# Second attention: high and low parts of queries and keys stacked on the 32 rows of one single-pass product, spread by transfers into three buffers

## The chip, the cores and the metric

The kernel runs on one core of one Trainium2 chip. The metric is the device time of one execution in microseconds; lower is better. The engines named below are TensorE (PE; its weight loads are shown apart as PEld), VectorE (DVE), ScalarE (ACT), GpSimd (POOL) and SyncE (SP), which here only issues transfers.

## The reference, cut to what matters

The whole program is two transformer-like layers over 8 batches of 256 tokens of width 128. The change touches the attention of the second layer alone:

```python
H, HD, R, QK = 16, 8, 8, 32
xn = _ln(x, g1, b1)
q = _lin(xn, Wq, bq).reshape(b, n, H, HD) / np.sqrt(HD)
k = _lin(xn, Wk, bk).reshape(b, n, H, HD)
score = jax.nn.softmax(jnp.einsum('bihd,bjhd->bhij', q, k), axis=-1)
v = _lin(xn, Wv, bv).reshape(b, n, R, HD)
out = jnp.einsum('bhij,bjrd->bihrd', score, v)
comp = softmax([qv, out] @ Ws.T + bs, axis=3)      # over the 8 value heads
out = (comp * out).sum(axis=3)
```

There are 16 query heads of only 8 features. So a score product contracts over 8 numbers, while the array has 128 rows.

## The kernel before, in words

The program is a row of stages; a barrier of all engines stands between two of them. The stage in question (here "the second attention") begins at about 584.7 us and ends at about 834 us of the profile. The stage ahead of it is that of the mixture of experts (from 453 us) with the layer norms that follow it (to 584 us).

**Heads and rows.** `Q` holds the projected queries of a batch, 128 rows by 256 tokens: four groups of 32 rows, each with the 8 features of four heads. `KZ` holds the keys four times, each copy with only one head of every group left and the others made zero (scale and bias columns `QT`, `BS`, L1276 to L1279). A score product of head k takes the 32 rows `rows_of(k)` (group k % 4) of `Q` and of copy k // 4 of `KZ`, so it contracts over 32 rows of which 8 count. All these operands are plain float32; every such matmul appears in the profile as two instructions. `MR`, `SEL` are rounded float32 (fp32r) and a matmul of them is one instruction.

**Two products per head.** L2164 ("max") computes the scores with queries on the partitions; DVE takes the maximum over the keys from it (L2312). L2161 ("exp") computes them transposed, and L2169 subtracts the maximum in the same bank (`SEL` picks the head's row of `MR`); ACT takes the exponential into `PT` (L2225). L2201 then multiplies the four 128x128 pieces of `PT` of each head by `VXT` (64 value columns, 8 score columns, a column of ones); ACT copies the result to `UB` (L2238).

**The order of the work** is written out by hand and is the same on each engine (`batches`, `turn`). A batch has eight steps i = 0 to 7. In step i PE issues `scores(i)`: the exp products of heads 2i, 2i+1 of batch b and the max products of two heads of batch b+1, interleaved; after it, from i = 1 on, `weighted(i - 1)`, the 16 instructions of L2201 for two heads. After step 7 come `project_next` (queries and keys of batch b+2 from `TR` and `WQK`, L1270; ACT then makes `Q` and `KZ`), `weighted(6)`, `turn_max` (two transposes of `M4`, L2186, which DVE copies to `MR`, L2326) and `weighted(7)`. A first round with no batch to finish (`b = None`) does the maxima of batch 0 only; the last one has no maxima. DVE, besides the maxima, does for the batch before the "finish" steps: start (step 0), end (step 2, after ACT's exponential of `CM`, L2245), weigh (steps 3, 4, L2293) and sum (steps 5, 6, L2299). After the last maximum of a batch DVE rounds and splits the maxima (`MH`, `M4`, L2316 to L2320), which `turn_max` waits for.

**Banks.** `UP_` (banks 0 to 3: max, projection, turn) and `UM` (banks 4 to 7: exp, weighted) are rings: a use waits until the engine that reads the use four places earlier is done. `keep_busy` (L295) issues identity products on PE: three ahead of the first scores, four after the first `turn_max`.

**The stage ahead of it** folds the norm's gain and shift into `WQK` and the bias columns (L1913 to L1950), and in its last waves ACT and DVE run norms by turns, after which PE turns, projects values (L1852) and projects batch 0 (L1270); ACT makes `Q`, `KZ` of batch 0 as its last work there (L1909).

Of the kernel before, what the change touches and what calls it, by code (L numbers as in the profile page):

```python
# [21 lines left out]
P = 128  # L22
# [151 lines left out]
def build(nc, x_in, pa_in, pb_in, pc_in, pd_in, out_dram):  # L174
# [4 lines left out]
    with ctx:  # L179
# [1076 lines left out]
        s4 = ctx.enter_context(ExitStack())  # L1256
        VXT = sbuf(s4, "VXT", [P, NT, VX])
        CT = sbuf(s4, "CT", [P, NT, H2])
        BS = sbuf(s4, "BS", [P, 5])
# [3 lines left out]
        Q = [sbuf(s4, f"Q{n}", [P, L]) for n in range(2)]  # L1263
        KZ = [sbuf(s4, f"KZ{n}", [P, 4, L]) for n in range(2)]
# [9 lines left out]
        def take_projections(bank, odd):  # L1274

            nc.scalar.activation(Q[odd][:, :], bank[:, 0:L], ACT.Identity, bias=BS[:, 4:5], scale=1.0 / math.sqrt(HD2))  # L1276
            for s_ in range(4):
                last = nc.scalar.activation(KZ[odd][:, s_, :], bank[:, L:2 * L], ACT.Identity, bias=BS[:, s_:s_ + 1],
                                            scale=QT[:, s_:s_ + 1])  # L1279
            return last  # L1280

        sb = ExitStack()
        with sb:
# [440 lines left out]
            sba.close()  # L1724
            XBT = sbuf(sb, "XBT", [P, SLOTS * P])
# [11 lines left out]
            BX = sbuf(sb, "BX", [P, 2])  # L1737
            PROD = sbuf(sb, "PROD", [P, 4 * 64])
# [11 lines left out]
            c_turned, c_copied, c_proj, c_qk0 = sem("c_turned"), sem("c_copied"), sem("c_proj"), sem("c_qk0")  # L1750
# [20 lines left out]
            with nc.Block() as block:  # L1771
                @block.sync
                def _(sp):
                    sp.wait_ge(moe_stored, 16 * SLOTS)
                    for g in range(NG):
                        own = slice(4 * g, 4 * g + 4)
                        sp.dma_start(MO[:, own, :], by_token[0:NT * P, :].rearrange("(t p) c -> p t c", p=P)[:, own, :])\
                            .then_inc(moe_back[g], 16)

                @block.gpsimd  # L1780
                def _(pool):
                    nc.gpsimd.memset(BD[:, :, :], 0.0).then_inc(c_zero, 1)
                    nc.gpsimd.memset(VXT[:, :, VX - 1:VX], 1.0).then_inc(c_zero, 1)
                    pool.wait_ge(loadC, 16)
                    for n, w in enumerate(("wq", "wk")):
                        nc.gpsimd.tensor_copy(WQK[:, n * P:(n + 1) * P].rearrange("p (j s d) -> p j s d", j=4, s=4),
                                              one_part(pc(w))).then_inc(c_wqk, 1)
# [9 lines left out]
                def _(pe):  # L1797
# [3 lines left out]
                    last.then_inc(c_cols, 1)  # L1801
                    pe.wait_ge(c_bd, 1)
# [41 lines left out]
                    pe.wait_ge(c_ready, 2)  # L1844
                    for g in range(NG):
# [10 lines left out]
                        if g == 0:  # L1856
                            project(PS[:, 0, :], 0).then_inc(c_qk0, 1)

                @block.scalar
                def _(act):  # L1860
# [49 lines left out]
                    act.wait_ge(c_qk0, 1)  # L1910
                    take_projections(PS[:, 0, :], 0)

                @block.vector  # L1913
                def _(dve):
# [13 lines left out]
                    V.link(nc.vector.tensor_copy(SEL[:, :], CRW[:, :]))  # L1928
                    dve.wait_ge(c_cols, 1)
# [833 lines left out]
```

## Time and profile before

| what | us |
|---|---|
| times of three runs | 1008.54 (median), 1008.1, 1018.52 |
| the profiled execution, its own time | 1008.61 |
| its span, first to last instruction | 1006.9 |
| the second attention, steps of batches 0 to 7 | 608.5 to 823.2 |
| mean granted TensorE clock over the span | 0.813 |

The span leaves out 1.7 us of the profiled execution's time. Busy time of an engine is the union of its instructions. In a line of the timeline, several instructions of one kind in a row are merged (xN); "[idle before <- releaser]" is how long the engine had waited and what ended it. The granted clock is 1.0 at 2.4 GHz and 0.5 at 1.2 GHz.

### The profile page before, as it was taken

The numbers are of one execution on the slowest core, as the hardware profiler recorded it, in microseconds if no ns is written. First come the engines' busy times: TensorE is split into PE (matmuls) and PEld (weight loads), VectorE is DVE, ScalarE is ACT, GpSimd is POOL, SyncE is SP. The second block draws the span as 40 slices with busy tenths as digits, with TensorE's granted clock in tenths as the row PEclk, the third lists the DMA queues.
The fourth block names the chain that finished last, engine by engine and source line by source line (L and its number), as shares of the span: only waits on it lengthen the run. The fifth ranks groups of instructions, "written<-read, shape, count | busy, mean of one in ns | idle before, by whom it ended". The sixth has DMA issues, their size and how long they took to land. (4 is left out here: it accounts for less than half of the span.)

```text
span 1006.9 us, 15707 instructions
## 1 busy us (share of the span) xinstructions
PE 742.9 (74%) x5853; PEld 608.8 (60%) x5853; DVE 589.5 (59%) x1330; ACT 446.8 (44%) x920; POOL 84.6 (8%) x96
## 2 busy tenths in 40 slices
PE   3993869998932695518940479999999974759986
PEld 2443769995432475418840347888888864538765
DVE  4119999983484363413327543777777657575574
ACT  3332526453534454203534614555555533446554
POOL 0002203000001101061420020000000001000000
PEclk9996757697955788557985569999999986869989
DMA  5200260005001000021020030000000000000000
GB/s 166 33 0 1 41 105 1 1 3 220 26 1 64 1 1 1 1 68 46 31 63 0 0 118 1 2 2 1 0 1 1 2 1 1 0 1 1 1 22 21
DMA packets 27457, 26.43 MB, mean 26 GB/s; under 512 B 17424, under 2 KB 25488, under 8 KB 26624
## 3 DMA queue, kind: packets, MB, share of 16 engines
q1 hardware_dynamic: 26144, 22.99, 8.0%
q0 software_dynamic: 1248, 2.57, 0.8%
q8 instruction: 42, 0.69, 0.3%
q14 instruction: 23, 0.19, 0.1%
HBM read 20.32 MB, written 5.23 MB: 25 GB/s over the span
## 5 line engine op out<-in xcount | busy, mean ns | idle before, releaser
L2201 PE MATMUL PS<-VXT,PT 128*128 128x73 f32 (+1 forms) x1024 | 126.6, 277 | 4.8 <-ACT PT L2225 4.8
L2201 PEld LDWEIGHTS PS<-VXT,PT 128*128 128x128 f32 x1024 | 119.7, 192 | 17.0 <-issue 12.3
L2312 DVE TENSOR_REDUCE MX<-PS 128x2 f32<-128x512 f32 x128 | 81.7, 686 | 47.5 <-PE PS L2164 46.8
L2225 ACT ACTIVATE PT<-PS 128x512 f32<-128x512 f32 x128 | 68.6, 597 | 47.4 <-PE PS L2169 47.4
L2161 PE MATMUL PS<-Q,KZ 32*128 32x256 f32 x512 | 76.8, 397 | 0.0
L2164 PE MATMUL PS<-KZ,Q 32*128 32x256 f32 x512 | 72.8, 409 | 1.9 <-DVE MX L2312 1.7
L2169 PE MATMUL PS<-MR,SEL 32*128 32x256 f32 x256 | 58.8, 462 | 0.0
L2238 ACT ACTIVATE UB<-PS 128x292 f32<-128x292 f32 x64 | 26.6, 415 | 52.8 <-PE PS L2201 52.8
L2164 PEld LDWEIGHTS PS<-KZ,Q 32*128 32x128 f32 x512 | 45.1, 190 | 5.3 <-DVE MX L2312 4.1
L404 PE MATMUL PS<-XT,WT 128*128 x96 | 42.3, 595 | 1.0 <-ACT XT L290 1.0
L2161 PEld LDWEIGHTS PS<-Q,KZ 32*128 32x128 f32 x512 | 38.8, 184 | 5.7 <-issue 0.8
L1876 ACT ACTIVATE HT<-PS,PB 128x128 f32<-128x128 f32 x92 | 26.2, 368 | 24.9 <-PE PS L1834 20.8
L2538 ACT ACTIVATE PB<-PS,PB 128x512 f32<-128x512 f32 x48 | 31.8, 685 | 4.2 <-PE PS L2451 4.2
L2642 DVE TENSOR_TENSOR HBL<-PB,HBH 128x512 fp32r<-128x512 f32 x32 | 22.1, 692 | 19.3 <-ACT PB L2538 18.8
L2293 DVE TENSOR_TENSOR UP<-UB,CM 128x1024 f32<-128x1024 f32 x16 | 32.0, 2010 | 0.1
L384 DVE COPY QTK<-PS 128x512 f32 x4 | 2.8, 692 | 49.1 <-PE PS L415 49.1
L404 PEld LDWEIGHTS PS<-XT,WT 128*128 128x128 f32 x96 | 17.7, 188 | 22.7 <-issue 22.7
L2461 PE MATMUL PS<-HBH,WR 128*128 128x512 f32 x64 | 28.2, 441 | 3.7 <-DVE HBL L2642 3.7
L1848 PE MATMUL PS<-PB,NRM 128*128 128x128 f32 x16 | 4.4, 429 | 32.9 <-ACT NRM L1896 32.9
L1839 PE MATMUL PS<-PB,HT 128*128 x184 | 25.5, 281 | 4.0 <-ACT HT L1876 3.8
L1834 PE MATMUL PS<-XBT,W1C 128*128 128x128 f32 x184 | 27.0, 294 | 1.3 <-DVE W1C L1966 1.1
L2461 PE MATMUL PS<-HBL,WR 128*128 128x512 f32 x64 | 27.2, 425 | 0.0
(465 smaller groups left out, 1778.3 us busy)
## 6 DMA issues: line engine op xcount, KB each, us to landing
PB<-in_pb SPq DMA_DIRECT2D x1, 5016.0 KB, 17.7
PB<-in_pd SPq DMA_DIRECT2D x1, 2888.0 KB, 9.8
X<-in_x SPq DMA_DIRECT2D x2, 1024.0 KB, 4.8
X<-fir_rows SPq DMA_DIRECT2D x2, 1024.0 KB, 6.5
TR<-fir_rows SPq DMA_DIRECT2D x2, 1024.0 KB, 8.7
PA<-in_pa SPq DMA_DIRECT2D x1, 1731.0 KB, 8.5
PC<-in_pc SPq DMA_DIRECT2D x1, 1560.0 KB, 6.4
by_expert<-ZERO_ SPq DMA_DIRECT2D x1, 1483.5 KB, 15.7
```

The costliest lines, as they stand in the source:

```text
L404: last = nc.tensor.matmul(PS[:, p, :].rearrange("p (b l) -> p b l", b=2), WT[:, p, j, :], XT[:, bass.ds(g * 2, 2), j:j + L], start=(j == 0 ...
L1834: last = nc.tensor.matmul(bank[:, c * P:(c + 1) * P], W1C[:, j % 2, c * P:(c + 1) * P], XBT[:, j * P:(j + 1) * P], start=True, stop=True)
L2161: nc.tensor.matmul(PS[:, UM.bank(at_m[("exp", k)]), os], KZ[odd][rows_of(k), k // 4, cs], Q[odd][rows_of(k), :], start=True, stop=False)
L2164: last = nc.tensor.matmul(PS[:, UP_.bank(at_p[("max", k)]), os], Q[even][rows_of(k), cs], KZ[even][rows_of(k), k // 4, :], start=True, sto ...
L2169: last = nc.tensor.matmul(PS[:, UM.bank(at_m[("exp", k)]), os], SEL[rows_of(k), k:k + 1].to_broadcast([32, P]), MR[odd][rows_of(k), :], st ...
L2201: last = nc.tensor.matmul(PS[:, UM.bank(n), col:col + VX], PT[:, k % 4, c, f * P:(f + 1) * P], v, start=(c == 0), stop=(c == 1))
L2225: nc.scalar.activation(PT[:, k % 4, :, :], PS[:, UM.bank(n), :].rearrange("p (c q) -> p c q", c=2), ACT.Exp).then_inc(c_act, 1)
L2238: nc.scalar.activation(UB[odd][:, 2 * u:2 * u + 2, :, :].rearrange("p h f c -> p (h f c)"), PS[:, UM.bank(n), 0:4 * VX], ACT.Copy).then_in ...
L2293: nc.vector.tensor_tensor(UP[:, half, :, :], ub[:, half, 0:64].rearrange("p a (r d) -> p a d r", r=R2), cm[:, half, :].unsqueeze(2).to_bro ...
L2312: nc.vector.tensor_reduce(MX[:, :, k], PS[:, UP_.bank(n), :].rearrange("p (f q) -> p f q", f=2), AX.X, ALU.max, negate=True).then_inc(p_dv ...
L2461: last = nc.tensor.matmul(bank, pdr(kind)[:, at:at + P], src[:, s_, k, :], start=(k == 0 and m == 0), stop=(k == 3 and m == 1))
L2538: nc.scalar.activation(FF[:, s_, c, :], bank, func, scale=pd(scale)[:, c:c + 1])\
```

## The change

- `Q` and `KZ` go. `HALVES` holds four planes of 128 x 256: the high part (a rounding to fp32r) and the low part (the rest) of the queries, and the same two of the keys. ACT makes the high parts (`high_parts`, two ACTIVATE), DVE the low parts (`low_parts`, two SCALAR_TENSOR_TENSOR that read the bank and the high part).
- `spread`: SP copies them by 32 transfers a batch (SBUF to SBUF, 32 KB each: 32 rows of 1 KB to 8 partitions of 4 KB) to `Q4` and `K4`, three buffers of each by b % 3. There each head has 32 rows: 8 features times the four combinations high/low of queries with high/low of keys. So one fp32r product over the 32 rows is the score.
- The max and exp products take `Q4`, `K4`; each is one instruction in place of two.
- The projection of batch b+2 moves from after step 7 to after `scores(0)`; ACT's part follows in step 0, DVE's in step 1; they share bank 2 with the maxima, and the max product that next takes that bank (one of step 2) waits for both parts.
- The loop over batches (`Fori`) is written out.
- In the stage ahead: a permutation of the features (`PERM` by POOL, one more product, three small DVE operations ahead of `c_cols`, some after the fold taken away), PE waits for `c_bias` and `c_perm` before the products of `BD`. The parts of batch 0 are made in wave 4 (ACT after `turned(1)`, DVE after `values(0)`), spread by SP in that stage, and no longer at its end.

```diff
+        def high_parts(act, bank, b):
+            act.wait_ge(split_full, b + 1)
+            if b:
+                arrived(act, b - 1)
+            for s_ in range(2):
+                nc.scalar.activation(HALVES[:, 2 * s_, :], bank[:, s_ * L:(s_ + 1) * L], ACT.Identity,
+                                     bias=BS[:, s_:s_ + 1]).then_inc(split_high, 1)
+
+        def low_parts(dve, bank, b):
+            dve.wait_ge(split_high, 2 * b + 2)
+            for s_ in range(2):
+                nc.vector.scalar_tensor_tensor(out=HALVES[:, 2 * s_ + 1, :], in0=bank[:, s_ * L:(s_ + 1) * L],
+                                               scalar=BS[:, s_:s_ + 1], in1=HALVES[:, 2 * s_, :], op0=ALU.add,
+                                               op1=ALU.subtract).then_inc(split_low, 1)
+
+        def spread(sp, b):
+            sp.wait_ge(split_high, 2 * b + 2)
+            sp.wait_ge(split_low, 2 * b + 2)
+            for to, plane_of in ((Q4, lambda c: c // 2), (K4, lambda c: 2 + c % 2)):
+                for g in range(4):
+                    for c in range(4):
+                        at = 32 * g + 8 * c
+                        sp.dma_start(to[b % 3][at:at + 8, :, :].bitcast(F32),
+                                     HALVES[32 * g:32 * g + 32, plane_of(c), :].bitcast(F32)).then_inc(split_in[b % 4], 16)
...
+                    pe.wait_ge(c_bias, 1)
+                    pe.wait_ge(c_perm, 1)
+                    nc.tensor.matmul(PS[:, 3, 8:10], PERM[:, :], BC[:, :],
+                                     start=True, stop=True)
                     pe.wait_ge(c_bd, 1)
...
-                    act.wait_ge(c_qk0, 1)
-                    take_projections(PS[:, 0, :], 0)
+                        if w == NORMS + 1:
+                            high_parts(act, PS[:, 0, :], 0)
...
+                        if w == NORMS + 1:
+                            low_parts(dve, PS[:, 0, :], 0)
...
-            prep = ROUND + [("qk", 0), ("turn", 0)]
+            prep = ROUND[0:2] + [("qk", 0)] + ROUND[2:] + [("turn", 0)]
...
+                for b in [None] + list(range(B)):
+                    after = 0 if b is None else b + 1
+                    last = after == B
                     for i in range(H2 // 2):
+                        scores(i, b, None if last else after)
+                        if i == 0 and after + 1 < B:
+                            project_next(after + 1)
+                        if i == 1 and after + 1 < B:
+                            split_next(after + 1)
...
+                    for b in range(1, B):
+                        if b >= 3:
+                            UM.wait_full(sp, b - 3, at_m[("exp", H2 - 1)])
+                        spread(sp, b)
...
+                        if maxes:
+                            if i == 0:
+                                arrived(pe, a)
                             for k in maxes:
-                                UP_.wait_empty(pe, a, at_p[("max", k)])
+                                n = at_p[("max", k)]
+                                UP_.wait_empty(pe, a, n)
+                                if n == at_p[("qk", 0)] + 4 and a + 1 < B:
+                                    pe.wait_ge(split_high, 2 * a + 4)
+                                    pe.wait_ge(split_low, 2 * a + 4)
...
-                                nc.tensor.matmul(PS[:, UM.bank(at_m[("exp", k)]), os], KZ[odd][rows_of(k), k // 4, cs],
-                                                 Q[odd][rows_of(k), :], start=True, stop=False)
+                                nc.tensor.matmul(PS[:, UM.bank(at_m[("exp", k)]), os], K4[b % 3][rows_of(k), k // 4, cs],
+                                                 Q4[b % 3][rows_of(k), k // 4, :], start=True, stop=False)
```

## Rows read from the trace of the kernel before

**Rows 1.** The page's second part: TensorE's granted clock in 40 slices of the span
```profile
PEclk9996757697955788557985569999999986869989
```

**Rows 2.** Busy time by stretch (us, instructions, then clock, DMA share, GB/s): batches 0, 4, 7
```profile
608.50:636.70 28.20, 26.47 (x299) 23.86 (x298) 11.26 (x20) 14.86 (x29) 0.00 (x0) 1.00 0.01 2
...
717.00:743.70 26.70, 26.31 (x295) 23.70 (x294) 20.35 (x33) 14.36 (x30) 0.00 (x0) 1.00 0.00 0
...
797.30:823.20 25.90, 25.23 (x225) 22.44 (x224) 9.64 (x13) 12.19 (x25) 0.00 (x0) 1.00 0.00 1
```

**Rows 3.** Timeline of PE (start, us, what): one step, and a batch's end
```profile
701.19 0.48 PE L2161 MATMUL PS<-Q,KZ 32*128 32x256 f32 x2
...
701.51 0.38 PE L2161 MATMUL PS<-Q,KZ 32*128 32x256 f32 x2
...
701.54 0.47 PE L2169 MATMUL PS<-MR,SEL 32*128 32x256 f32 x2
...
702.48 2.01 PE L2201 MATMUL PS<-VXT,PT 128*128 x16
704.42 0.48 PE L2161 MATMUL PS<-Q,KZ 32*128 32x256 f32 x2
...
712.18 1.13 PE L1270 MATMUL PS<-TR,WQK 128*128 x4
...
714.89 0.38 PE L2186 MATMUL PS<-PB,M 128*128 128x128 f32 x2
...
716.94 0.48 PE L2161 MATMUL PS<-Q,KZ 32*128 32x256 f32 x2
```

**Rows 4.** Timeline of DVE across the turn from one batch to the next
```profile
712.20 1.29 DVE L2312 TENSOR_REDUCE MX<-PS 128x2 f32<-128x512 f32 x2 [0.82 <-PE PS L2164]
...
713.88 0.29 DVE L2320 TENSOR_TENSOR M<-MX,MH 128x128 f32<-128x128 f32 x1
...
718.25 1.29 DVE L2312 TENSOR_REDUCE MX<-PS 128x2 f32<-128x512 f32 x2 [2.52 <-PE PS L2164]
...
721.69 2.48 DVE L2312 TENSOR_REDUCE MX<-PS 128x2 f32<-128x512 f32 x4
725.60 0.42 DVE L2282 TENSOR_REDUCE RI<-CM 128x32 f32<-128x256 f32 x1 [1.44 <-ACT CM L2245]
...
727.01 1.28 DVE L2312 TENSOR_REDUCE MX<-PS 128x2 f32<-128x512 f32 x2
```

**Rows 5.** Timeline of ACT: the exponential of CM in the same batch
```profile
725.16 0.41 ACT L2245 ACTIVATE CM<-CM 128x256 f32<-128x256 f32 x1
```

**Rows 6.** SP's issues in the timeline, and an issue group (KB each, us to landing)
```profile
519.89 2.01 SPq L1777 DMA_DIRECT2D MO<-by_token  x4
```
```profile
fir_rows<-FROW SPq DMA_DIRECT2D x1, 96.0 KB, 1.6
```

**Rows 7.** Timeline rows of the stage ahead: PE at its start, ACT in its waves
```profile
454.09 1.89 PE L1804 MATMUL PS<-BD,PC 128*128 128x16 f32 x8
```
```profile
566.34 0.49 ACT L1896 ACTIVATE OB<-X,NMG,R2S 128x128 f32<-128x128 f32 x1 [1.12 <-DVE NMG L2007]
```

**Rows 8.** Stretches chosen for the clock (PE busy first, clock after POOL)
```profile
114.40:138.30 23.90, 23.90 (x227) 23.90 (x226) 21.91 (x59) 5.12 (x14) 0.17 (x1) 0.50 0.75 131
554.80:558.30 3.50, 3.50 (x12) 3.09 (x13) 0.07 (x1) 3.50 (x10) 0.00 (x0) 0.50 0.01 2
...
592.30:595.70 3.40, 3.09 (x24) 2.05 (x22) 3.31 (x6) 0.00 (x0) 1.50 (x3) 1.00 0.10 41
595.70:602.50 6.80, 6.68 (x29) 4.73 (x28) 4.93 (x9) 0.00 (x0) 3.90 (x3) 0.50 0.01 2
...
821.00:824.40 3.40, 2.19 (x20) 2.04 (x19) 0.70 (x2) 0.83 (x2) 0.00 (x0) 1.00 0.00 0
```

**Rows 9.** Timeline of PE at the lower clock: value products and a projection
```profile
554.78 2.00 PE L1852 MATMUL PS<-WVE,TR 128*128 128x80 f32 x8 [8.37 <-ACT TR L1883]
556.57 1.99 PE L1270 MATMUL PS<-TR,WQK 128*128 128x256 f32 x4
```

More of the change, by code:

```diff
@@ L2095, in turn @@
                         if i and i < LAST:
-                            weighted(i - 1, b, odd)
-                        if not first:
+                            weighted(i - 1, b)
+                        if b:
                             for u in finish.get(i, ()):
-                                finish_step(u, b - 1, 1 - odd)
-                    if b is None:
-                        project_next(0, 1)
-                        turn_max(0, 0)
-                        return
-                    if not last:
-                        project_next(b + 1, odd)
-                    weighted(LAST - 1, b, odd)
-                    if not last:
-                        turn_max(b + 1, 1 - odd)
-                    weighted(LAST, b, odd)
-                return turn
-            def every_batch(eng, turn):
-                turn(None, 0)
-                turn(0, 0, first=True)
-                with eng.Fori(0, (B - 4) // 2) as i:
-                    turn(i * 2 + 1, 1)
-                    turn(i * 2 + 2, 0)
-                for b in range(B - 3, B):
-                    turn(b, b % 2, last=b == B - 1)
+                                finish_step(u, b - 1)
+                    if b is not None:
+                        weighted(LAST - 1, b)
+                    if not last:
+                        turn_max(after)
+                    if b is not None:
+                        weighted(LAST, b)
                 for steps in finish.values():
                     for u in steps:
-                        yield u
+                        finish_step(u, B - 1)
+            nothing = lambda *_: None
             with nc.Block() as block:
@@ L2208, in _, with scores @@
                     keep_busy(UM.bank(0), pc("wq"), 3)
-                    for _ in every_batch(pe, batches(scores, project_next, turn_max, weighted, lambda *_: None)):
-                        pass
+                    every_batch(scores, project_next, nothing, turn_max, weighted, nothing)
                 @block.scalar
                 def _(act):
-                    def scores(i, now, after):
-                        if now is None:
+                    def scores(i, b, a):
+                        if b is None:
                             return
-                        b, odd = now
                         for k in (2 * i, 2 * i + 1):
@@ L2245, in finish_step @@
                             nc.scalar.activation(CM[:, :, :], CM[:, :, :], ACT.Exp).then_inc(c_e, 1)
-                    UP_.open(act, "A")
                     UM.open(act, "A")
-                    for u in every_batch(act, batches(scores, project_next, lambda *_: None, weighted, finish_step)):
-                        finish_step(u, B - 1, 1)
+                    every_batch(scores, project_next, nothing, nothing, weighted, finish_step)
                 @block.vector
```

131 lines of the change are left out of this document (66 added, 65 removed).

## The prediction

> **What bounds the kernel now.** I read the clock by slices first, then busy time by batch, then the timelines of PE, DVE and ACT over one batch, then the clock in chosen stretches. Through the second attention the clock is granted in full (the 9s of slices 25 to 32 [rows 1]; 1.00 by batch [rows 2]). A middle batch takes 26.8 us: PE is busy 26.31, DVE 20.35, ACT 14.36 [rows 2]. So PE bounds it, and DVE is the next, closer than 6 us suggests: it has waits that no faster PE removes. A PE step is 3.23 us (701.19 to 704.42): 1.29 for the burst of score products, 1.94 for the 16 instructions of the weighted product [rows 3]. Only the burst gets shorter.
>
> **The burst.** The records of one 32-row group end at 701.67 (first instruction of the exp product), 701.89 (second) and 702.01 (L2169, the single-pass one) [rows 3]: 0.22 us for each plain instruction, 0.12 for a rounded one. A group carries twice 0.22 + 0.22 + 0.12 = 1.12; the other 0.17 of the 1.29 is start and change of shape. After: 4 x 0.12 + 0.17 = 0.65. The max group goes from four plain instructions (0.88) to two rounded (0.24), so the first maximum is ready 0.64 earlier: DVE begins 1.31 after the burst's start now (716.94, 718.25) [rows 3, 4], then 0.67. PE's own work for a batch becomes 8 x (0.65 + 1.94) + 0.97 (projection) + 0.3 = 22.0 us.
>
> **A middle batch at full clock.** t = 0 is the start of burst 0. DVE: first maxima 0.67; to the next maxima, with the finish start between, 3.44 (718.25 to 721.69) [rows 4]: 4.11; those two 1.21, at 5.32. New here: two operations of 128x256. ACT's and DVE's operations of that size take 0.41 to 0.43 [rows 4, 5] and overlap a little, together 0.8 (bounds: 0.6, one short pass each, and 1.3, two whole reduces of 512 columns): 6.1. Burst 2 waits for them, since its max product shares bank 2. PE would otherwise be there at 0.65 + 0.97 + 0.65 + 1.94 = 4.2, so it idles about 1.9 us and starts at 6.2. Now burst 2 starts at 716.94 + 2 x 1.29 + 1.94 = 721.46 and the reduction of CM, released by ACT, comes 4.14 later [rows 4, 5]; with the shorter burst 3.5, at 9.7. From there to the maxima of step 3 it is 1.41: 11.1. From those to the maxima of step 7 DVE takes 712.20 + 26.8 - 727.01 = 12.0 now, 0.82 of it waiting for PE [rows 4]; that wait goes: 11.2, at 22.3. The last maxima and M4 take 1.97 (712.20 to 714.17): 24.2. PE has finished weighted(6) at 21.9 and waits 2.4 us. The transposes and weighted(7) take 2.05 (714.89 to 716.94) [rows 3]: the next burst 0 starts at 26.4. So a middle batch goes from 26.8 to 26.4: DVE becomes the bound, and PE stands still twice, 1.9 and 2.4 us.
>
> **The ends.** In batch 0 DVE has no finish work and in batch 7 no maxima; PE stays the bound. Batch 0: 28.1 [rows 2] less 8 x 0.64 is 23.1. Batch 7: 25.9 to 20.8. The Fori written out changes nothing that I see.
>
> **ACT and SP.** ACT drops five operations and gains two: about 1.4 us less, off the path; the exponentials of step 1 come behind them, before PE asks for them. SP issues 32 transfers. The four of rows 6 stand 0.55 apart at the end, single ones last 0.33 to 0.4; they carry 512 rows each, these 32, so I take 0.42: 13.4 us; landing 1.6 as for 96 KB [rows 6] (bounds 0.35 and 0.55; landing 1.6 and 3.7): 15 us, 12.8 at best, 21.3 at worst. From 6.1 they land at 21, needed at 26.4; at worst 27.4, 1.0 late in each middle batch. In the first round the parts of batch 1 are ready near 594, landing near 609, where burst 0 of batch 0 now starts (608.5): +0.8 (bounds -0.7, +5).
>
> **The stage ahead.** PE's products of BD started at 454.09 [rows 7]; they now wait for three DVE operations that end near 455.8 and for one product more. That chain leads to the experts' first tile: +2 (0 to +3). In wave 4 two ACT and two DVE operations enter the ring ACT-DVE-ACT; ACT's idle 1.12 [rows 7] covers the first, the DVE pair is late by about +1 (0 to +2). The end of that stage loses ACT's five operations, which DVE's last values outlast anyway: 0.
>
> Sum at full clock: +2 +1 +0.8 -5.0 -6 x 0.4 -5.1 = -8.7.
>
> **The clock.** What decides is whether PE keeps 2.4 GHz. Before, PE was busy 95% and more of every middle batch with the clock at 1.00. The other stretches show what light work does. From 592.3 to 595.7 PE worked 3.09 of 3.40 us, but on 32-row products of two groups with short waits for DVE between; the clock fell to 0.50 at 595.7 and stayed there to 602.5 though PE was busy 6.68 of 6.80. From 821.0 to 824.4 it issued the last weighted products, 2.19 of 3.40 busy, and the clock fell. From 554.8 to 558.3, busy throughout with the value products (80 columns, the nearest form to L2201) and a projection, it did not rise; from 114.4 to 138.3, busy without a break on products of 64 columns, it did not rise in 24 us [rows 8]. After the change each middle batch has two stops of 1.9 and 2.4 us between weighted products, which is like the stretch at 821. I take it that the clock falls at the first stop, in batch 1, and that what follows (short rounded bursts, weighted products) is of the kind that did not raise it.
>
> At the lower clock the eight value products take 1.79 (554.78 to 556.57), and the projection's record is 1.99 against 1.13 at the higher, so 1.8 from start to start [rows 3, 9]; so 16 weighted instructions take 3.5 (3.6, less for 73 columns), a burst 4 x 0.24 + 0.17 = 1.1, the turn 0.5. A batch: 8 x 4.6 + 1.8 + 0.5 = 39.1, bound by PE, with no stop left. Batch 0 stays high, 23.1. Batch 1 falls near t = 6: 6.2 + 6 x 1.1 + 7 x 3.5 + 0.6 = 37.9. Batches 2 to 6: 195.5. Batch 7: 36.6. Together 293.1 against 28.1 + 6 x 26.8 + 25.9 = 214.8: +78.3. With the +3.8 of the other stages the profiled execution's 1008.6 (span 1006.9 and 1.7 around it; the median run, 1008.5, is the same) goes to 1090.7; I say 1090. If the clock falls in batch 0 already, at the wait for the first exponentials, it is 15 more; each batch in which it rises again for a time gives back about 11. Own range: 1062 to 1110.
>
> **Rivals.**
> 1. The clock holds. For it: the stops are short, and it held through batch 0, where PE stood still 28.20 - 26.47 = 1.7 us [rows 2]. Against it: 592 to 596 and 821 to 824 [rows 8]. Time: 1008.6 - 8.7 = 1000, not slower. The Trainium skill (TensorE: Matmul & The Clock Gate, Why this matters for your kernels) asks only that idle gaps stay below a length that neither stop here reaches; by that rule this rival would be the outcome, 1000. The trace does not agree: the clock fell at 595.7 with at most 0.31 us idle in the stretch before it.
> 2. It falls at each stop but soon rises. Each fall doubles some 1.2 us of PE work on DVE's path: about 27.7 a batch, sum -5.0 + 5.4 - 5.1 + 3.8: 1008. With transfers that land late (1.0 a batch and 5 at the start) it is 1018, the same kind of result. Against it: no light work raised the clock in the stretches above [rows 8]. The same page of the Trainium skill (What's actually happening) has PE's activity alone release the clock, which would make this the outcome once it has fallen, 1008; the trace does not agree, with 23.90 us busy out of 23.90 at 0.50.
> 3. It rises in about every second batch, with the projection between two bursts: 3 x 11 less, 1057; 1025 to 1062 in all.
>
> **How the numbers follow.** Forecast (stays low) 0.60; rival 3 0.15; rival 2 0.10; rival 1 0.15. About 1% is what a measurement of this kernel tells from no change (998.5 to 1018.6). Faster: half and a bit of rival 1, 0.09. Same: the rest of it and most of rival 2, 0.14. Slower: 0.77. The range leaves out rival 1 below, so it begins at 1005; above it takes in a fall in batch 0: 1110.
>
> **What would show it.** Right: a granted clock near 0.5 from some 610 to 640 us on to the end of the stage; L2201 at about 0.22 us apart; batches of 39 us; DVE waiting for PE at L2312. Also, whatever the clock: bursts of 0.65 at 2.4 GHz; in a batch at full clock, PE held at burst 2 by DVE's low parts and at the transposes by M4; SP's 32 issues in some 13 us. Wrong: a clock of 1.00 through the middle batches (then the sum at full clock is what to check, 26.4 a batch), or PE waiting for transfers at burst 0.

## The result, and the profile after

The changed kernel takes 1135.7 us, median of 4 runs (1132.3 to 1144.8), the kernel before 1009.2 beside it: ratio 1.125 (1.119 to 1.131), 126 us slower. 1090 was predicted, with 1110 as the upper end. The direction and the cause in the large (TensorE's clock) were right; the size was 46 us short. The profiled execution took 1136.6, span 1134.8. A ratio here and below leaves out slow runs (more than 1.5% above the fastest of their own kernel), while a median counts every run.

The granted clock in 40 slices, for [rows 1]:

```profile
PEclk9997567889567955697556555555555555768989
```

From slice 23 to slice 34 it is half; these slices are the second attention. Stretches of it, in the columns of [rows 2]: batch 0, a middle batch, batch 7, and one more from where the clock fell to where it rose:

```profile
630.20:670.50 40.30, 40.22 (x230) 36.77 (x230) 12.13 (x22) 13.61 (x26) 0.00 (x0) 0.50 0.08 27
710.80:751.10 40.30, 40.30 (x231) 36.75 (x230) 21.38 (x35) 13.14 (x27) 0.00 (x0) 0.50 0.08 27
911.00:949.30 38.30, 37.64 (x193) 34.97 (x192) 9.64 (x13) 12.19 (x25) 0.00 (x0) 0.50 0.00 1
...
624.80:966.20 341.40, 323.46 (x1826) 296.88 (x1827) 161.26 (x258) 106.91 (x216) 0.00 (x0) 0.50 0.06 20
```

A middle batch takes 40.3 us with PE busy for all of it, against 26.8. All eight batches are at 1.2 GHz, batch 0 too. One step, as in [rows 3]:

```profile
723.56 0.58 PE L2199 MATMUL PS<-SPLIT 32*128 32x256 f32 x2
...
724.71 3.69 PE L2238 MATMUL PS<-VXT,PT 128*128 128x73 f32 x16
728.33 0.58 PE L2199 MATMUL PS<-SPLIT 32*128 32x256 f32 x2
```

The burst takes 1.15 and the 16 weighted instructions 3.62, a step 4.77 (3.23 before). The costliest groups of the page (busy, mean ns, then idle before and its releaser):

```profile
L2238 PE MATMUL PS<-VXT,PT 128*128 128x73 f32 x1024 | 234.6, 421 | 0.7 <-ACT PT L2260 0.7
...
L2342 DVE TENSOR_REDUCE MX<-PS 128x2 f32<-128x512 f32 x128 | 82.0, 686 | 129.4 <-PE PS L2202 129.4
```

The reader sees that DVE's own work is unchanged (82.0 us) and that it waits 129.4 us for PE. Why batch 0 was late and cold stands in the timelines of SP and of PE (rows as in [rows 6] and [rows 3]):

```profile
571.42 22.85 SPq L1300 DMA_DIRECT2D SPLIT<-SPLIT  x32
595.00 0.36 SPq L2161 DMA_DIRECT2D PB<-in_pd  x1
605.00 23.21 SPq L1300 DMA_DIRECT2D SPLIT<-SPLIT  x32
```

```profile
595.36 5.46 PE L295 MATMUL PS<-PC,PB 128*128 128x512 f32 x6 [7.75 <-PEq L1798]
600.75 0.57 PE L2202 MATMUL PS<-SPLIT 32*128 32x256 f32 x4
...
605.07 0.92 PE L2202 MATMUL PS<-SPLIT 32*128 32x256 f32 x8 [2.25 <-DVE SPLIT L1289]
...
614.41 5.38 PE L295 MATMUL PS<-PC,PB 128*128 128x512 f32 x8
630.28 0.58 PE L2199 MATMUL PS<-SPLIT 32*128 32x256 f32 x2 [10.48 <-DMA SPLIT<-SPLIT]
```

32 issues on SP take 22.9 us, 0.71 each. Those of batch 0 end at 594.3, when ACT and DVE had been done for 5 us (DVE's last row there ends at 589.2), and hold the barrier until 595.3. Those of batch 1 end at 628.2. PE waits 10.5 us for them behind its identity products, and in this wait the clock, which these had raised (at 618.0), falls (at 624.8).

The span is 127.9 longer. 10.7 of it stand up to the barrier (584.67 against 595.36): 2.0 are there before the first product of the stage ahead, 3.4 lie between that product and DVE's last row (583.83 against 589.18), and 5.3 are the barrier's wait for SP. PE's first row of the stage ahead, before and after:

```profile
453.13 0.98 PE L1800 MATMUL PS<-PB,PC 128*128 128x1 f32 x4 [21.78 <-PEq L1358]
```

```profile
455.11 0.99 PE L1830 MATMUL PS<-PB,PC 128*128 128x1 f32 x4 [21.92 <-PEq L1379]
```

The rest: 11.1 from the barrier to burst 0 of batch 0 (23.8 against 34.9), 104.3 from that burst to the last weighted product (608.5 to 823.2 against 630.3 to 949.3: 214.7 and 319.0), 1.8 behind it.

### The profile page after: what moved, and what is told of

Same layout as the page of the kernel before. It is cut to its first block and busy times, and to the rows that moved or that the text cites. A ratio compares the mean times of both kernels' runs of the same rounds, so it can differ in the third digit from the quotient of the medians.

```text
span 1134.8 us, 14637 instructions
## 1 busy us (share of the span) xinstructions
PE 849.4 (75%) x5339; PEld 706.5 (62%) x5339; DVE 596.8 (53%) x1348; ACT 434.9 (38%) x891; POOL 85.1 (7%) x97
## 5 line engine op out<-in xcount | busy, mean ns | idle before, releaser
L2238 PE MATMUL PS<-VXT,PT 128*128 128x73 f32 x1024 | 234.6, 421 | 0.7 <-ACT PT L2260 0.7
L2238 PEld LDWEIGHTS PS<-VXT,PT 128*128 128x128 f32 x1024 | 223.4, 330 | 13.2 <-issue 12.1
L2342 DVE TENSOR_REDUCE MX<-PS 128x2 f32<-128x512 f32 x128 | 82.0, 686 | 129.4 <-PE PS L2202 129.4
L2199 PE MATMUL PS<-SPLIT 32*128 32x256 f32 x256 | 63.2, 493 | 11.2 <-DMA SPLIT<-SPLIT 10.5
L2199 PEld LDWEIGHTS PS<-SPLIT 32*128 32x128 f32 x256 | 39.4, 305 | 23.4 <-issue 15.5
L2202 PE MATMUL PS<-SPLIT 32*128 32x256 f32 x256 | 49.6, 488 | 4.8 <-DVE MX L2342 2.5
L2207 PE MATMUL PS<-MR,SEL 32*128 32x256 f32 x256 | 52.9, 411 | 0.0
L2207 PEld LDWEIGHTS PS<-MR,SEL 32*128 32x128 f32 x256 | 42.3, 328 | 0.0
L2202 PEld LDWEIGHTS PS<-SPLIT 32*128 32x128 f32 x256 | 31.4, 303 | 7.9 <-DVE MX L2342 6.3
L2425 POOL TENSOR_TENSOR OB<-OB,PC 128x1024 f32<-128x1024 f32 x2 | 4.7, 2342 | 369.1 <-ACT NRM L2520 369.1
```

What stands on the lines that cost most here:

```text
L2199: nc.tensor.matmul(PS[:, UM.bank(at_m[("exp", k)]), os], K4[b % 3][rows_of(k), k // 4, cs], Q4[b % 3][rows_of(k), k // 4, :], start=True, ...
L2202: last = nc.tensor.matmul(PS[:, UP_.bank(at_p[("max", k)]), os], Q4[a % 3][rows_of(k), k // 4, cs], K4[a % 3][rows_of(k), k // 4, :], star ...
L2207: last = nc.tensor.matmul(PS[:, UM.bank(at_m[("exp", k)]), os], SEL[rows_of(k), k:k + 1].to_broadcast([32, P]), MR[b % 2][rows_of(k), :], ...
L2238: last = nc.tensor.matmul(PS[:, UM.bank(n), col:col + VX], PT[:, k % 4, c, f * P:(f + 1) * P], v, start=(c == 0), stop=(c == 1))
L2342: nc.vector.tensor_reduce(MX[:, :, k], PS[:, UP_.bank(n), :].rearrange("p (f q) -> p f q", f=2), AX.X, ALU.max, negate=True).then_inc(p_dv ...
```

## The experiments

Two theories stood first: the loop itself cannot hold the clock (A), or only the late transfers took it (B). An identity product is one call of `keep_busy`: 512 columns in two instructions, 0.9 us at 2.4 GHz (one of them ahead of each burst took a step from 2.60 to 3.51 us). Single times are given beside the kernel before in the same comparison, since its median moved between 1009 and 1016. A single execution also carries a shift from ahead of the changed code: the stage ahead begins at 453.1 us in the profile before, at 463.5 in that of the kernel before without its four identity products (equal up to there), and between 450.4 and 465.4 in the other profiles. So some 10 us of a single time say nothing; the clock, the batches and the waits in its trace do.

**The term that was mis-sized, taken out.** Half of the transfers go to POOL's queue, in every round.

```diff
-            for to, plane_of in ((Q4, lambda c: c // 2), (K4, lambda c: 2 + c % 2)):
+            for to, plane_of in [((Q4, lambda c: c // 2), (K4, lambda c: 2 + c % 2))[half]]:
...
-                        spread(sp, b)
+                        spread(sp, b, 0)
...
+                    spread(pool, 1, 1)
```

> The changed kernel with one edit: every round of transfers is divided between SP (queries) and POOL (keys), 16 each. The identity products stand where the change has them, there is no filler. This takes out the term of the prediction that was mis-sized (issues of 0.42 us each, measured 0.70) and leaves the rest. Theory A (with transfers in time the prediction's course holds): barrier not held up, PE reaches batch 0 within 2 us of the end of the four identity products and at clock 1.0, batch 0 in 23 us, the clock falls at the first stops of batch 1 and stays at 0.50: 80 us over the kernel before, 1088 to 1098 us. Rival B (late transfers were the whole of it): within 10 us of the kernel before.

1094.6 us (1083.2 to 1101.2), before 1015.0, ratio 1.072 (1.065 to 1.080); profiled span 1095.7. That is A's time: 80 us over the kernel before. PE's timeline at the end of batch 0 and in batch 1, then a later batch in the columns of [rows 2]:

```profile
635.49 0.38 PE L2209 MATMUL PS<-SPLIT 32*128 32x256 f32 x2
...
637.88 2.01 PE L2248 MATMUL PS<-VXT,PT 128*128 128x73 f32 x16
641.67 0.39 PE L2209 MATMUL PS<-SPLIT 32*128 32x256 f32 x2 [1.79 <-DVE SPLIT L1293]
...
642.34 2.51 PE L2248 MATMUL PS<-VXT,PT 128*128 128x73 f32 x16
...
645.93 3.69 PE L2248 MATMUL PS<-VXT,PT 128*128 128x73 f32 x16
```

```profile
711.90:752.20 40.30, 40.30 (x232) 36.75 (x231) 21.37 (x35) 13.13 (x27) 8.57 (x16) 0.50 0.17 27
```

Theory A, row by row: batch 0 runs from 612.41 to 635.49 at full clock, 23.1 us. In batch 1 PE stands still for 1.79 us at burst 2, which starts 6.2 us into the batch, and the next 16 products already take 2.51, then 3.69. The clock stays low to the end of the stage. A run with the same division and nine identity products in the wait ahead of batch 0 gave the same:

> The changed kernel with every round of transfers divided between two queues (queries on SP, keys on POOL, which took 0.55 us for each before), and the four identity products replaced by nine that fill PE's wait ahead of batch 0. No filler in the bursts. Theory A (the stops that DVE causes, at burst 2 and at the turn, are enough to lose the clock): PE no longer waits for transfers anywhere, batch 0 at 1.0 in 23.1 us, then the clock falls in batch 1 and stays at 0.50, batches of 40: 1095 to 1115 us. Rival B (in the kernel with the moved products it was the wait for late transfers at the start of batch 1 that ended the clock, not DVE's stops): the clock stays at 1.0, middle batches of 26.0 to 26.8 us, 1005 to 1015 us.

1101.3 us (before 1016.3): the fall at 654.5, batches of 40.3, and once, at 811.5, a rise for 20 us. It ended at 832.0, in a stop of 2.23 us at the turn.

**The clock given back, transfers still late.**

```diff
-                        if p == 0:
-                            keep_busy(UM.bank(0), pc("wq"), 4)
...
                                 arrived(pe, a)
+                                if a == 1:
+                                    keep_busy(UM.bank(0), pc("wq"), 4)
```

> The changed kernel with the four identity products moved: no longer behind the first transposition of maxima, but directly ahead of the first burst of batch 0, behind its wait for the transfers. Theory A (the lateness of the first transfers only put the clock down early; the changed loop cannot keep it, and the first stop of PE in batch 0 or 1 ends it): granted clock 1.0 for less than two batches from about 633, then 0.50; 1110 to 1130 us. Rival B (the long wait ahead of batch 0 was the only cause; the changed loop keeps a clock it was given): clock 1.0 to the end of the stage, a batch of 26.4 to 27 us, stage end near 855 instead of 960, so 1028 to 1036 us.

1138.2 us (before 1012.6): full clock in batch 0 (644.3 to 667.4, 23.2 us), lost at 670.6 during the next wait for transfers, and never back. The time is 8 us above A's range. Batch 0 began 14 us later than in the changed kernel, but 8.2 of them are the shift ahead of the changed code (463.3 against 455.1); the rest is about the time of the products, and only one batch was saved. It did not tell A from B, since the fall came in a wait for transfers; the run above does.

**Does the loop before get it back?** The kernel before, without the four identity products behind its first turn:

```diff
-                        if isinstance(p, int) and p == 0:
-                            keep_busy(UM.bank(0), pc("wq"), 4)
```

> The kernel before, without its four identity products behind the first transposition of maxima; nothing else differs and nothing of the computation is left out. Theory A (the clock that the second attention starts with is kept, since its own products never bring it back): the granted clock stays at 0.50 from about 600 on through the whole stage; the step becomes 2.6 us of burst (1.29 twice) and 3.6 of weighted products, 6.2 us, so a batch some 50 us against 26.8, and the kernel 1008 + 150 to 190 = 1160 to 1200 us. Rival B (the products of the loop bring the clock back by themselves within a batch): 1008 to 1030 us.

1039.2 us (before 1012.6). The cold stretch and a middle batch:

```profile
620.50:663.90 43.40, 42.05 (x271) 36.48 (x263) 10.93 (x19) 14.19 (x28) 0.00 (x0) 0.54 0.00 1
...
692.00:718.80 26.80, 26.41 (x296) 23.78 (x296) 20.38 (x34) 14.40 (x32) 0.00 (x0) 1.00 0.00 1
```

A missed: the loop before came back to 1.00 at 663.9 by its own products, after one batch (and for 4 us at 622.5, early in that batch). The time is above B's range too, by 9 us; 10.4 of the difference to the profile before are the shift. So the change took away two things, the hold and the return.

**Is it the short bursts?** The changed kernel with divided transfers, each score product issued twice, with the same result:

```diff
                             for k in maxes:
+                                nc.tensor.matmul(PS[:, UP_.bank(at_p[("max", k)]), os], Q4[a % 3][rows_of(k), k // 4, cs],
+                                                 K4[a % 3][rows_of(k), k // 4, :], start=True, stop=True)
                                 last = nc.tensor.matmul(
```

> As the changed kernel with its transfers divided between SP and POOL (1094.6 us), and every score product (32 rows, single pass) issued twice, the second overwriting the first; waits, order and transfers as there, no filler. Theory A (the loop loses the clock because its bursts have become short: PE has too little to do between and around the stops): the burst becomes 1.05 to 1.1 us at full clock, the stop at burst 2 shrinks to 0.6 and that at the turn to 1.5; the clock stays at 1.0 through most batches, middle batches 26.4 to 27.5: 1010 to 1030 us. Rival B (the new waits and the 32-row single-pass form lose it, however many are issued): clock 0.50 from batch 1 or 2 on, step 1.9 + 3.6 = 5.5 us, 45 us a batch: 1125 to 1145 us.

1060.0 us (before 1016.1), between the ranges of the two theories:

```profile
650.50:688.10 37.60, 37.60 (x254) 34.63 (x256) 18.88 (x30) 11.53 (x24) 8.09 (x16) 0.50 0.18 29
688.10:718.80 30.70, 27.92 (x347) 25.41 (x343) 24.01 (x41) 15.04 (x32) 9.48 (x18) 1.00 0.23 37
718.80:756.40 37.60, 37.60 (x257) 34.41 (x256) 18.96 (x32) 11.28 (x24) 7.67 (x15) 0.50 0.18 28
```

With more work in the bursts the clock comes back (688, 756), and goes again each time after a batch with stops (PE idle 2.8 us of 30.7). So it is with the short bursts that the clock does not return, as far as one execution shows; that it falls is down to the stops together with what surrounds them, and doubling did not cure that.

**Work in every burst.** The clock given back, and one identity product ahead of each burst:

```diff
+                        if exps:
+                            keep_busy(UM.bank(at_m[("exp", 2 * i)]), pc("wq"), 1)
```

> As the run with the moved identity products, and one more identity product (512 columns in two instructions, 0.43 us at 2.4 GHz, written to a bank that the following product starts anew) ahead of every burst of batches 0 to 7. Theory A (what the changed loop lacks is work on PE, not time): the clock holds at 1.0 through the stage, the 0.43 us lie in PE's slack of a DVE-bound batch (82 us of maxima on DVE; step near 3.3), batch 26.5 to 27.5, in all 1028 to 1040 us. Rival B (the stops at the second burst and the turn end it whatever else PE does): clock 0.50 after one or two batches, step 4.8 + 0.9 = 5.6 us, 1160 to 1190 us.

1080.5 us (before 1012.6). The clock was mostly 1.0 (it fell four times in the stage), but a batch took 32 to 35 us. I had put an identity product at 0.43; it adds 0.9 to the step, so PE became the bound at 3.51, and PE waited for transfers at the start of batches (1.46 at 699.1). With divided transfers for the first two batches only:

> As the run with the filled bursts, and the transfers of the first two batches divided between two queues: those of queries on SP, those of keys on POOL for batch 0 and on ACT for batch 1. Theory A (the queue that issues, at 0.70 us each, sets when the first two batches can start): SP's part of batch 0 takes 11.5 instead of 23 us and ends before the rest of the stage ahead (589), if POOL issues one in under 1 us; the barrier falls at 590 instead of 595 and PE's wait ahead of batch 0 goes from 10.5 us to nearly none: 10 to 16 us less than the run with the filled bursts alone. Rival B (landing, not issuing, is the limit): within 4 us of it.

1067.7 us, 12.7 less, as A said (by the traces more, since this execution carries 6.6 us more of the shift). With all of them divided, nine identity products ahead of batch 0, and 256 columns in place of 512:

> As the run without filler, and one identity product of 256 columns (0.43 us at 2.4 GHz) ahead of every burst of batches 0 to 7. Theory A (PE needs more work, spread over the batch; 0.65 + 1.84 + 0.43 = 2.9 us a step stays below DVE's share): clock 1.0 throughout but for single short falls, middle batches 26.4 to 27.2 us, 1008 to 1020 us. Rival B (the fillers must stand in the stops themselves): clock falls in batch 1 or 2 and comes back only in part, 1040 us or more.

1045.8 us (before 1016.3):

```profile
654.90:682.40 27.50, 26.04 (x254) 21.95 (x248) 21.18 (x35) 13.06 (x27) 8.58 (x16) 1.00 0.14 40
745.60:783.20 37.60, 37.60 (x196) 32.08 (x195) 16.72 (x26) 9.98 (x21) 6.83 (x13) 0.50 0.17 26
```

The hold lasted four batches of 27.5 us or less; the fifth, in which the clock fell behind a stop of 1.35 us, took 43. The time is B's, though the clock fell later than B had it: the bursts are not the place.

**Work in the stops.** Divided transfers and nine identity products ahead of batch 0, as in the run before, and two identity products where PE stands still anyway:

```diff
+                        if exps and maxes and i == 2 and a + 1 < B:
+                            keep_busy(UM.bank(at_m[("exp", 2 * i)]), pc("wq"), 2)
...
+                        if p:
+                            UM.wait_empty(pe, p - 1, at_m[("out", LAST)])
+                            keep_busy(UM.bank(at_m[("out", LAST)]), pc("wq"), 2)
                         pe.wait_ge(c_m4, p + 1)
```

> As the run without filler, and two identity products of 512 columns (0.86 us each at 2.4 GHz) in each of the two stops of a batch only: ahead of the wait for the low parts at burst 2, and ahead of the wait for M4 at the turn. Theory A (the stops are what loses the clock): it stays at 1.0, and the fillers cost nothing since PE waited there: middle batches of 26.4 us, 1005 to 1015 us. Rival B (the light steps between the stops, 0.65 of 32-row products in 2.6 us, lose it): it falls within a few batches and comes back late or not, 1040 to 1110 us.

1034.2 us (before 1016.3):

```profile
682.70:708.80 26.10, 25.73 (x242) 21.23 (x239) 21.05 (x35) 12.95 (x27) 8.58 (x16) 1.00 0.26 42
812.50:848.30 35.80, 35.67 (x176) 33.37 (x176) 8.34 (x10) 10.68 (x22) 0.00 (x0) 0.50 0.00 0
```

The clock held from 624.7 to 812.5 and the middle batches took 26.1: the fillers cost nothing there. They are as much work a batch as in the run before (four products of 512 columns, there eight of 256), so it is the place that counts: the stops are where the changed loop loses the clock. The time lies between the two theories, with 12 us of the shift in it (465.4 against 453.1). Batch 7 has no maxima, no stop filled, and was lost. The nine products ahead of batch 0 lasted until 629.8, 6 us or more past the last transfer. Both mended:

> As the run with fillers in the two stops, with two corrections: four identity products ahead of batch 0 instead of nine (the nine outlasted the transfers by some 5 us), and one identity product of 256 columns ahead of each burst of batch 7, where the clock fell at its start and cost 16 us. Theory A: clock 1.0 from batch 0 to the end of batch 7, batch 7 in 24 to 25 us instead of 38; 17 to 19 us less than that run, so 0.5 to 7 us below the kernel before (ratio 0.993 to 1.000). Rival B (one product of 256 columns is too little where no maxima are computed): the clock falls in batch 7 again and it takes 38 us and more: ratio 1.010 to 1.020.

1027.1 us, ratio 1.014 (1.009 to 1.019). Batch 7 took 24.0 at full clock, but in the profiled execution batch 6, which computes no low parts, took 39.5 with the clock at 0.50 for most of it. The run before had the same batch 6 and kept its clock there, so the two executions do not show what decides it. With one product in each stop instead of two:

> As the run with four identity products ahead of batch 0 and filled stops, but one product of 512 columns in each stop instead of two. Theory A (the stop has to be filled nearly whole, 1.9 and 2.4 us): the clock falls within a few batches, 40 us more than the run with two. Rival B (half a filler is enough): within 3 us of the run with two.

1034.4 us, ratio 1.020 (1.013 to 1.027): the clock fell at 661, 712 and 767, each time 2 to 3 us behind a stop of 0.9 or 1.2, and then held from 778 to the end of the stage past stops of the same length. Half a filler is not a hold; in time it costs 7 us against the run with two, within the noise of both, where A had 40 and B at most 3. And with batch 6 filled as batch 7:

```diff
-                        if exps and not maxes:
+                        if exps and (not maxes or a + 1 == B):
                             nc.tensor.matmul(PS[:, UM.bank(at_m[("exp", 2 * i)]), 0:256], ident, pc("wq")[:, 0:256], start=True,
                                              stop=True)
```

> As the run with filled stops and a filled batch 7, with the 256-column product ahead of every burst of batch 6 too, which computes no low parts and so had only one filled stop. Theory A (batch 6 was the one place left where the clock fell in the profiled execution, at 770, for 39 instead of 26 us): clock 1.0 from batch 0 to the end of the stage, 12 us less than that run, ratio to the kernel before 0.998 to 1.006. Rival B (the hold is a matter of luck in every batch, and moves to another): the times spread over 15 us, some batch in the profiled execution is at 0.50, ratio 1.010 to 1.020.

1016.0 us, before 1016.4, ratio 0.998 (0.995 to 1.002). The twelve times spread over 15 us (1005.7 to 1020.5), and so do those of the kernel before (1008.9 to 1020.9). Batches 0, 2, 6 and 7:

```profile
621.20:648.30 27.10, 26.22 (x252) 21.91 (x252) 12.34 (x23) 13.90 (x27) 8.57 (x16) 1.00 0.23 41
674.10:700.20 26.10, 25.72 (x246) 21.23 (x240) 21.05 (x35) 12.96 (x28) 8.58 (x16) 1.00 0.26 42
778.50:805.30 26.80, 26.65 (x248) 21.89 (x248) 20.42 (x34) 12.30 (x25) 0.00 (x0) 1.00 0.01 1
805.30:829.50 24.20, 24.17 (x206) 20.59 (x206) 9.63 (x13) 11.89 (x24) 0.00 (x0) 1.00 0.00 1
```

The clock is 1.00 from the start of batch 0 to the end of batch 7, and the 126 us are gone with the arithmetic and the transfers of the change all in place.

**What the queue costs at full clock.** The last kernel with all 32 transfers on SP:

> As the run with filled stops and filled batches 6 and 7 (1016.0 us), but all 32 transfers of a round on SP. Theory A (at 0.70 us an issue a round takes 22.9 us and lands 1.6 later, from low parts that stand ready some 7 us into a batch; the next burst 0 waits for it): middle batches of 31 to 32 us instead of 26.1, a wait of 4 to 5 us in front of each burst 0, clock partly at 0.50 because of these waits, first batch 9 to 15 us later: 1055 to 1090 us. Rival B (the queue keeps up at full clock): 1025 to 1035 us.

1082.9 us (before 1016.1). PE ahead of a burst 0:

```profile
689.46 1.91 PE L2246 MATMUL PS<-VXT,PT 128*128 128x73 f32 x16
697.47 0.58 PE L2206 MATMUL PS<-SPLIT 32*128 32x256 f32 x2 [6.10 <-DMA SPLIT<-SPLIT]
```

The wait is 6.1 us and comes at every second batch (5.1 and 5.5 us the next times), with the clock at 0.50 for some 13 us behind it: turns stand 26 to 27 and 36.9 us apart in turn, 31.7 on the mean. A had this mean, but with a wait in front of each batch. At 40 us a batch the same queue keeps up, so the changed kernel shows none of this.

**What an issue costs.** On SP of the kernel before, idle in this stage, 8 unused transfers of each form:

```diff
+                    for rows, of, to in ((32, 256, 8), (32, 256, 32), (8, 1024, 8), (128, 256, 128), (128, 256, 32)):
...
+                            sp.dma_start(SPARE[r:r + to, c:c + wide], SPARE[0:rows, 0:of]).then_inc(spare_in, 16)
```

> The kernel before, and on SP, idle during the second attention, 5 groups of 8 unused SBUF to SBUF transfers behind the load of the weights: 32 rows of 1 KB to 8 rows of 4 KB (the change's form), 32 to 32 rows of 1 KB, 8 to 8 rows of 4 KB, 128 to 128 rows of 1 KB, 128 rows of 1 KB to 32 rows of 4 KB. Theory A (what an issue on SP costs follows the number of rows that are read or written, not the bytes): 0.70 for the first and second, less for 8 rows, more for 128. Rival B (every issue costs the same, 0.35 to 0.42, and the 0.70 came from the wait on landing or from a full queue): all groups near 0.4. The time stays within 3 us of the kernel before, since PE and DVE touch none of it.

1008.1 us. SP's timeline, first, second, third and last form:

```profile
586.63 5.88 SPq L2139 DMA_DIRECT2D SPARE<-SPARE  x8
...
595.97 5.01 SPq L2139 DMA_DIRECT2D SPARE<-SPARE  x8
...
602.23 5.35 SPq L2139 DMA_DIRECT2D SPARE<-SPARE  x8
...
616.86 5.14 SPq L2139 DMA_DIRECT2D SPARE<-SPARE  x8
```

0.73, 0.63, 0.67 and 0.64 us each. Both theories missed: the price hardly depends on form, rows or bytes (the last form carries 128 KB, the first 32), and it is some 0.65 and not 0.4 for transfers from SBUF to SBUF, with the transfers of the group before landed at the start of each group.

**The rest of the way.** The bias product moved behind BD's, 4 of 32 transfers of batch 1 on ACT, the waits of the first round filled, three identity products ahead of batch 0 in place of four:

```diff
-                        spread(sp, b, 0)
+                        spread(sp, b, 0, range(3) if b == 1 else range(4))
...
+                        if not exps and i:
+                            keep_busy(UM.bank(0), pc("wq"), 2 if i == 2 else 1)
```

> As the run with filled stops and filled batches 6 and 7 (1016.0 us), with three mends: the product of the permuted biases stands behind the products of BD instead of ahead of them; ACT issues 4 of the 32 transfers of batch 1; PE fills its waits in the first round too (one identity product of 512 columns ahead of each burst, two at the low parts) and has three ahead of batch 0. Theory A (these are the remaining costs of the change: 2 us in the chain ahead, 4 us before batch 0): 5 to 7 us less, ratio to the kernel before 0.990 to 0.996. Rival B (the fillers of the first round delay the maxima as much as they save, and the stage ahead is bound by something else): ratio 0.997 to 1.003.

1020.1 us, ratio 1.008 (1.004 to 1.011), slower than without, and above the ranges of both theories. POOL and DVE in the first round:

```profile
606.97 5.39 POOL L2177 CAST WR<-PB 128x512 fp32r<-128x512 f32 x5
```

```profile
607.18 4.66 DVE L2370 CAST MH<-MX 128x32 fp32r<-128x32 f32 x1
```

A copy of 32 maxima took 4.66 us while POOL cast weights. With POOL's casts moved behind its transfers of batch 2:

```diff
+                    spread(pool, 2, 1)
                     pool.wait_ge(loadD, 16)
```

> As the run with the three mends, with POOL's five casts of weights moved behind its transfers of batch 2. In that run DVE's copy of the 32 maxima (0.20 us elsewhere) took 4.66 us at 607.2, while POOL cast weights from 607.0 to 612.4, and the granted clock fell during PE's wait of 7 us behind it. Theory A (the two stood in each other's way): the copy takes 0.2 us again, the turn comes 4.5 us earlier, the clock stays high up to batch 0: 5 to 8 us less than that run, ratio to the kernel before 0.990 to 0.998. Rival B (it was something else of the first round, such as ACT's issues): the copy is as long again, ratio 1.004 to 1.010.

1013.3 us, before 1016.4, ratio 1.000 (0.997 to 1.003): the copy is 0.18 again, as A said, and the ratio 0.8% better than in the run before, between the ranges of the two. No version beats the kernel before by more than can be measured.

## Why the prediction was right or wrong

**Right: the clock falls at the first stop of batch 1 and stays low.** The changed kernel itself does not show this, since its clock had fallen ahead of batch 0. In the run with divided transfers PE's stop is 1.79 (1.9 predicted), burst 2 starts 6.2 us into the batch (6.2), the clock goes there and stays for 283 us. The second stop, at the turn, shows in the run with the rise at 811.5: 2.23 (2.4 predicted). Filling the two stops keeps the clock at 1.00 where the same work in the bursts did not, which shows the cause.

**Failed: SP's 32 issues, "I take 0.42: 13.4 us", with 0.55 as the upper bound.** They take 0.71 each, 22.9 us. The estimate mixed issues of other kinds (from and to HBM); no row showed one from SBUF to SBUF, so the bounds should have been wider. The term stood at +0.8 and measured 15.8: 5.3 for the barrier that waits for SP's own queue, a wait that the prediction did not name at all, and 10.5 ahead of batch 0. This wait then put the clock down before batch 0. The prediction priced a fall there at "15 more", but for another wait, that for the first exponentials, and left it out of the sum: batch 0 took 40.3 instead of 23.1, 17.2. Together 15.0 and 17.2, 32 of the 46 us.

**Too small: the cold batch.** 39.1 was predicted, 40.3 measured: the 16 weighted instructions take 3.62 and not 3.5, and a burst 1.15 and not 1.1, eight times a batch. The loop without batch 0 is 278.7 against 270.0, 9 us. The products of 80 columns in [rows 9] gave 3.6; the forecast took something off for 73 columns, and the rows show nothing of that.

**The stage ahead** was +3 and came to 3.4, from its first product to DVE's last row; 2.0 more are there already before it begins, and are the shift that any execution carries. The chain of the bias product is the +2, and stands in PE's row (DVE's third bias operation is the releaser):

```profile
458.10 0.58 PE L1834 MATMUL PS<-BC,PERM 128*128 128x2 f32 x2 [2.00 <-DVE BC L1965]
```

**Right at full clock.** A middle batch was to go from 26.8 to 26.4 with DVE as the bound; it is 26.1 with fillers that lie in the stops. Batch 0 was to take 23.1 and took 23.1 where it began at full clock (the prediction's 28.1 for it before is 28.2 in the row, and 23.1 follows from that). The low parts cost 0.87 a pair (0.8). The loop was to lose 12.5 us; in the run with batches 6 and 7 filled it loses 6.4 (621.2 to 829.5 is 208.3, against 214.7), and the fillers of batches 0 and 7, where PE is the bound, account for 7.4 (27.1 for 23.1, and 24.2 for 20.8). So the gain was real, and holding the clock used up half of it. The other 6.4 went ahead of the loop: in that run the stage ahead takes 136.1 us from its first product to the barrier (131.5 before), and from there to batch 0 it is 25.5 (23.8), 6.2 us in all.

**The rivals.** Rival 1, the clock holds: no run of the changed loop without filler held it past a stop of 1.8 us. For holding a clock once gained, the Trainium skill (TensorE: Matmul & The Clock Gate, Why this matters for your kernels) bounds only the length of idle gaps; this one stayed below it and the clock fell, so the measurement decides against it here. Rival 2, it rises soon: true of the loop before (back after one batch) and, with doubled products, of the changed loop, but not of the changed loop as it is, busy 323.5 of 341.4 us at 0.50. The same page of the Trainium skill (What's actually happening) has activity alone release the clock; these rows do not agree. One of the rows that spoke against this rival was misread: the products of 114.4 to 138.3 are of 32 columns (128x32 in the timeline, on weights of 64 columns) and not of 64, so they are further from the weighted products than the prediction took them to be. Rival 3, a rise in every second batch: this is how the run with doubled products behaves (1060), and not the change.

## What to carry to other kernels

Fewer passes on PE are worth something only if PE stays busy: before one shortens PE's part, look at where it will stand still and what fills that place, since a stop of 2 us between light products cost this kernel 13.5 us a batch. Count a transfer's issues as work of the engine that issues them, at the price of the same kind of transfer, and look for the barrier behind them; dividing them between two queues took the ratio from 1.125 to 1.072 here. Filler work is free only inside the waits, and it has to be there in every batch, the last ones too.

## What was not expected of the hardware

- An SBUF to SBUF transfer costs SP some 0.63 to 0.73 us to issue, whether 32 or 128 KB; POOL issued the same transfers in 0.54 each (16 in 8.57 us).
- PE can be busy for all of 40.3 us and stay at 1.2 GHz, batch after batch, with 32-row single-pass products and 73-column products.
- DVE's copy of 128x32 within SBUF took 4.66 us beside POOL's casts and 0.18 without them, while DVE's reductions from PSUM beside POOL's casts in the kernel before kept their 0.64 us each. The Trainium skill (SBUF — State Buffer, SBUF: two separate sides) has GpSimd and some of DVE's instructions take turns at one pair of ports, held for a whole instruction. The trace agrees that the copy had to wait, but not that it was for one instruction: it began during the first of the five casts (two of them are of 128x2048 and take 1.9 each) and ended at 611.84, when the fourth ended (611.80).
- Stays open: which part of the work around the stops decides the fall. The kernel before stood still for 1.7 us in batch 0 and kept its clock; the changed loop with doubled bursts lost it behind stops of 1.0 to 1.5. The length of a stop alone does not decide either: with one product in each stop the clock fell behind some stops of 1.2 us and held behind others, and with two in each it was lost once (batch 6 of the run with filled stops and a filled batch 7) where no stop was longer than 0.8.
